# A state-space and expert layer on one Trainium2 core: five small moves in the order of a hand-scheduled loop

## The reference

```
h = layernorm(x) * (1 + ca) + sa
proj = h @ W_in.T;  x, gate = proj[:, :1024], proj[:, 1024:]
x = silu(conv_b + sum over 4 taps of conv_w * shifted x)
ssm = x @ W_x.T;  ts, B, C = rms(ssm[:, :32]), rms(ssm[:, 32:48]), rms(ssm[:, 48:])
dt = softplus(ts @ W_dt.T + b_dt)
state = state * exp(dt * A) + (dt * x) * B        # 1024 channels x 16 states, along the tokens
y = (sum over 16 states of state * C + x * D) * silu(gate);  out = y @ W_out.T
x = x + ga * out;  h = layernorm(x) * (1 + cb) + sb
x = x + gb * (h @ base_W.T + top-2 of 8 experts of rank 16)
```

## Time and profile before

| | |
|---|---|
| median of 3 runs | 1569.14 us (1564.22 to 1573.31) |
| the profiled execution's own time | 1564.21 us |
| its span | 1562.4 us |
| layer 1's recurrence, first to last scan | 536.4 to 1527.7 us of the span |
| granted PE clock, mean | 0.949 |
| busy share of the span, PE / DVE / ACT / POOL | 89% / 80% / 59% / 66% |

### The profile page before, as it was taken

The page is one execution under the profiler, slowest core; times in us unless marked ns, Lnnn a source line. Parts: engine busy times, 40 slices in busy tenths (PEclk is TensorE's granted clock), DMA queues, the critical chain, the costliest instruction groups (busy, mean ns, idle before and its releaser), DMA issues.

```text
span 1562.4 us, 25203 instructions
## 1 busy us (share of the span) xinstructions
PE 1384.7 (89%) x8789; PEld 995.4 (64%) x8789; DVE 1257.6 (80%) x1662; ACT 922.2 (59%) x2519; POOL 1038.6 (66%) x731
## 2 busy tenths in 40 slices
PE   6689999999999678699799899899899899988677
PEld 5467677767776467567567567567666666755543
DVE  4684674457344489999999999999999999999994
ACT  3332333223322677767877787787687777776651
POOL 0343242313223398888997997998898898899870
PEclk9699999999999889899999899999999999989589
DMA  9431222210001100200200110110020020020001
GB/s 326 163 109 55 88 83 74 66 38 20 29 28 33 68 14 1 82 1 15 68 28 15 55 42 1 56 54 1 24 86 1 14 96 1 1 68 28 1 0 41
DMA packets 32389, 77.17 MB, mean 49 GB/s; under 512 B 3667, under 2 KB 4723, under 8 KB 31750
## 3 DMA queue, kind: packets, MB, share of 16 engines
q1 hardware_dynamic: 32262, 75.55, 14.4%
HBM read 66.99 MB, written 8.55 MB: 48 GB/s over the span
## 4 chain that ended last, share of the span: by engine, by line
DVE 21%; PE 20%; POOL 10%; issue 9%; ACT 8%; DVEq 0%; ACTq 0%; POOLq 0%
DVE h L2212 12%; DVE acc L2228 6%; PE ps_h L1476 6%; POOL dbu L2024 5%; POOL h L2059 4%; ACT ps_a L1712 3%; PE ps_o L1500 2%; PE ps_m L1400 2%; ACT ab L1839 1%; PE ps_m L1440 1%; PE ps_h L1461 1%; PE ps_o L165 1%; PE ps_m L165 1%; DVE sg L2264 1%; PE ps_o L166 1%
## 5 line engine op out<-in xcount | busy, mean ns | idle before, releaser
L2212 DVE TENSOR_TENSOR_SCAN h<-ps_a,carry,dbu 128x512 f32<-128x512 f32 x512 | 626.3, 1266 | 14.5 <-ACT ps_a L1712 5.0
L2024 POOL TENSOR_TENSOR dbu<-dtu,b_all 128x1020 f32<-128x1020 f32 x256 | 598.6, 2358 | 27.1 <-DVE h L2212 27.1
L1712 ACT ACTIVATE ps_a<-dt,a_neg 128x256 f32<-128x256 f32 (+1 forms) x1024 | 443.2, 466 | 141.0 <-DVE h L2212 139.4
L1476 PE MATMUL ps_h<-ident,h 128*128 128x128 f32 x1536 | 228.3, 292 | 79.0 <-DVE acc L2228 66.9
L2228 DVE SCALAR_TENSOR_TENSOR acc<-ps_h,c_cur,acc 128x512 f32<-128x512 f32 x384 | 268.2, 738 | 9.9 <-PE ps_h L1476 9.4
L1476 PEld LDWEIGHTS ps_h<-ident,h 128*128 128x128 f32 x1536 | 183.8, 150 | 130.1 <-DVE h L2212 85.7
L714 POOL TENSOR_TENSOR hid_l<-hid,hid_h 128x256 f16<-128x256 f32 (+1 forms) x88 | 77.6, 885 | 156.2 <-ACT hid_h L605 156.1
L2059 POOL TENSOR_TENSOR h<-h,c_all 128x1024 f32<-128x1024 f32 x64 | 151.1, 2361 | 15.4 <-ACT carry L1732 15.4
L597 ACT ACTIVATE sil<-ps_gu 128x256 f32<-128x256 f32 (+1 forms) x88 | 34.0, 386 | 179.3 <-PE ps_gu L167 179.3
L165 PE MATMUL ps_m<-h_h,wi_h 128*128 128x256 f16 x432 | 119.1, 276 | 3.9 <-PEq L155 2.4
L166 PE MATMUL ps_m<-h_l,wi_h 128*128 128x256 f16 x432 | 118.6, 275 | 0.0
(11 more groups left out here) (392 smaller groups left out, 2864.0 us busy)
## 6 DMA issues: line engine op xcount, KB each, us to landing
b_all<-bt_scratch SPq DMA_DIRECT2D x32, 512.0 KB, 3.8
wm<-in_wmod SPq DMA_DIRECT2D x7, 1024.0 KB, 5.1
wo<-in_wmod SPq DMA_DIRECT2D x5, 1024.0 KB, 8.4
xa<-in_x SPq DMA_DIRECT2D x8, 512.0 KB, 4.5
stage<-in_W_in SPq DMA_DIRECT2D x4, 1024.0 KB
x_scratch<-x SPq DMA_DIRECT2D x8, 512.0 KB, 3.1
c_all<-bt_scratch SPq DMA_DIRECT2D x8, 512.0 KB, 6.1
x<-x_scratch SPq DMA_DIRECT2D x8, 512.0 KB, 3.6
```

The costliest lines, as they stand in the source:

```text
L1476: tr = pe.transpose(ps_h[:, t, j * P:(j + 1) * P], h[:, s % RING, j, t * P:(t + 1) * P], W["ident"][:])
L1712: ex = nc.scalar.activation(ps_a[:, j, j % 2:], dt[:, m, j % 2:], ACT.Exp, scale=a_neg[:, m, st:st + 1])
L2024: nc.gpsimd.tensor_tensor(dbu[:, s % AHEAD, :, 1:], dtu[:, :, 1:], b_all[:, st, 1:].unsqueeze(1).to_broadcast([P, DG, CH - 1]), ALU.mult). ...
L2212: nc.vector.tensor_tensor_scan(h[:, s % RING, two].rearrange("p j t -> p (j t)"), ps_a[:, two].rearrange("p j t -> p (j t)"), dbu[:, s % A ...
```

## The change

Nothing is added and nothing is removed; every instruction stays, in another place of its engine's program.

1. PE: `add_h` of the fourth weighed state moves in step 5 ahead of the output projection; `add_h` of the first weighed state of the second group moves in step 17 ahead of `turn_y` and W_x. (The fourth of the second group stays where it was.)
2. PE: gate tile 0 moves from step 17, ahead of W_x, to step 18, behind it and ahead of `turn_ss`.
3. PE: the first half of the base product of the experts (`experts(p, 0)`) moves from the middle of step 22 to the end of step 23, behind the turned states. In the last iteration it stays.
4. POOL: `rms_pow` moves ahead of the product of step 23.
5. ACT and DVE: `high` and `low` of `T3_AT` move one step earlier; in step 4 DVE's residual addition `add_out_projection(p, 0)` moves ahead of `make_sg(i, 6)` and of `low`.

```diff
-GA_AT = {17: (0,), 19: (1,), 28: (2, 3), 30: (4,), 31: (5,)}
+GA_AT = {18: (0,), 19: (1,), 28: (2, 3), 30: (4,), 31: (5,)}
-BASE_AT = {22: (0,), 24: (1,), 25: (2,), 26: (3,)}
+BASE_AT = {24: (1,), 25: (2,), 26: (3,)}
...
+                if s == JOIN_AT:
+                    add_h(i, KC - 1, first)
                 if p is not None and s:
                     for q in WO_AT.get(s, ()):
                         out_projection(p, q)
...
                 if n is not None:
                     for m in GA_AT.get(s, ()):
                         gate_tile(n, m)
+                if s == NS + 1:
+                    add_h(i, NS, first)
                 for m in YA_AT.get(s, ()):
                     turn_y(i, m)
...
-                if st in ADD_AT:
+                if st in ADD_AT and s not in (JOIN_AT, NS + 1):
                     add_h(i, s - st + ADD_AT[st], first)
...
                 if st == JOIN_AT + 2:
                     turn_h(i, s)
+                if p is not None and n is not None and s == NS + JOIN_AT + 2:
+                    experts(p, 0)
...
             if n is not None:
-                for t in at_slot(T3_AT, s):
+                for t in T3_AT.get(s, ()):
                     high(n - 1, t, S["t3_mm"], S["t3_hi"], h3_h, t3_bank(t))
...
                 db(i, s, first)
-                if n is not None and s == WX_AT + 6:
-                    rms_pow(n)
                 if s >= AHEAD - 1 and on_pool(s - (AHEAD - 1)):
                     weigh_h(i, s - (AHEAD - 1))
+                if n is not None and s == WX_AT + 5:
+                    rms_pow(n)
...
+                if p is not None and s == 4:
+                    add_out_projection(p, 0)
                 if s == 4:
                     make_sg(i, 6)
                 if n is not None:
-                    for t in at_slot(T3_AT, s, 2):
+                    for t in at_slot(T3_AT, s):
                         low(n - 1, t, S["t3_hi"], S["t3_lo"], h3_h, h3_l, t3_bank(t))
-                if p is not None and s == 4:
-                    add_out_projection(p, 0)
```

## The result

| | before | after |
|---|---|---|
| median of four runs each | 1570.34 us (1564.22 to 1573.31) | 1547.18 us (1545.25 to 1548.59) |
| ratio of the two, with its 95% interval | | 0.9865 [0.983, 0.99] |
| span of the profiled execution | 1562.4 us | 1544.7 us |
| granted PE clock, mean | 0.949 | 0.950 |

The kernel became faster by 1.35%. (The ratio is estimated from all runs; the quotient of the two medians is 0.9853.) Span against span it is 17.7 us, where the sum of the terms was 17.9.

The account below looks back on a forecast made before the run. DVE was taken as the bound, with only its idle time to win. The terms 10.5 + 4.2 + 1.4 + 1.8 = 17.9 us, taken off the median of 1569.1, gave 1551.2 us, range 1542 to 1567.

Parts of the forecast that it names:

- A: Steps 4 to 6, three moves: DVE's gaps of 1.44 us an iteration go, 10.5 us in all.
- B: POOL's power ahead of product 23: DVE no longer waits for the power, 4.2 us in all.
- C: Gate behind W_x, sum of state 16 ahead: W_x starts 0.2 us earlier an iteration, 1.4 us in all.
- D: Base product moved out of step 22: DVE's additions there wait less for PE, 1.8 us in all.
- All three moves are needed: Steps 4 to 6: moving `low` alone leaves most of its 1.27 us gap to the addition of step 4.
- A in iteration 0: Gap of 2.43 us before step 4's addition: 0.9 us won, since POOL's late weighed states hold the join.
- Both covers: Power ends about 872.2, before DVE arrives at 874.17; product 23 ends 1 us before scan 23 needs it.
- Covered, barely: PE's sum of state 17 would end at about 868.2, and the scan of step 21 needs it by 868.4.
- the 0.76 goes, and turning 22 at half clock gives some 0.25 back: Step 22: the addition's 0.76 us wait goes, and PE's half-clock turn of state 22 costs some 0.25 again.
- rivals 1 and 2: PE's clock stays low a little longer, 1557 us, chance 0.17; or PE bounds steps 23 and 24, 1581, 0.07.
- Rival 3: Gain taken back behind each gap, by POOL's weighing 19 or ACT in steps 4 to 6: 1564 us, chance 0.14.

Follow-up runs that it names:

- u_d: Changed kernel with the base product back in the middle of step 22; median 1545.82 us, ratio 0.9868 to the kernel before.
- u_a: Changed kernel with the fourth sum, residual addition, `high` and `low` of steps 4 to 6 put back; median 1560.11 us, ratio 0.9951 to the kernel before.
- u_b: Changed kernel with POOL's power behind the product of step 23 again; median 1553.70 us, ratio 0.9911 to the kernel before.
- u_c: Changed kernel with gate 0 and the sum of state 16 back in their old places; median 1548.98 us, ratio 0.9884 to the kernel before.
- a_sum: Kernel before with only the fourth sum moved ahead of the output projection in step 5; median 1559.59 us, ratio 0.9946 to the kernel before.
- u_lag: Changed kernel with only `high` and `low` one step later again; median 1551.08 us, ratio 0.9905 to the kernel before.
- a_lag: Kernel before with only `high` and `low` one step earlier; median 1572.22 us, ratio 1.0031 to the kernel before.
- d_22: Changed kernel with the base product one step earlier, at the end of step 22; median 1550.24 us, ratio 0.9894 to the kernel before.
- g_ud: Changed kernel with ACT's W_x copy between the decay halves of step 20 and the base product back in step 22; 1544.65 us, ratio 0.9866 to before.
- g_copy: Changed kernel with ACT's copy of W_x between the two halves of step 20's decays; median 1548.22 us, ratio 0.9874 to the kernel before.
- again: The changed kernel itself run once more, nothing changed; median 1550.22 us, ratio 0.9888 to the kernel before.

## Why the prediction was right, and where not

The forecast was 1551.2 us, in the range 1542 to 1567; 1547.18 was measured. The 4 us between come from the point it was counted from. The sum made 1546.3 for an execution like the one profiled, and 1546.5 is what the profiled one took. I then added the 4.9 us by which the median of before lay above its profiled execution; the median of after lies only 0.6 above its own.

Part by part, in us. The third column is read from the two traces: the waits of DVE at the places that a part is about, before less after. The last two are what undoing the part cost, in stretches of one profiled execution each:

| part | predicted | waits gone | undone: iteration 0 | undone: iterations 1 to 6 |
|---|---|---|---|---|
| A | 8.6 + 0.9 + 1.0 | 8.6 + 0.7 + 1.0 | 4.4 | 7.3 |
| B | 4.2 | 2.5 + 2.0 | 0.8 | 3.9 |
| C | 1.4 | 1.8 - 0.6 | -0.1 | 0.9 |
| D | 1.8 | -0.4 | (-0.4) | -1.1 |
| sum | 17.9 | 15.6 | 4.7 | 11.0 |
| before minus after | | 18.1 | 1.9 | 13.9 |

In "waits gone" the first number is iterations 1 to 6, the second iteration 0, the third iteration 7. D's -0.4 in iteration 0 is no cost of D, which has no instruction there; the changed kernel run again differs by as much.

The two ways of pricing do not agree, and the last two columns add up to 15.7 of 15.8 us by luck: 4.7 for 1.9 in one and 11.0 for 13.9 in the other. What undoing a part brings beside its own waits is, as far as the traces were followed, where the stretches at 1.2 GHz then fall, and POOL.

From iteration 7 to the end 1.0 was predicted and 2.3 came. A's 1.0 is there: the two waits of step 6 went from 0.75 and 1.07 us to 0.15 and 0.69. Undoing A, B or C costs 2.6 to 2.8 us there each time, and this is for the most part one place, the last output projection behind the last scan. In the changed kernel and in u_d no stretch at 1.2 GHz falls on it and it takes 7.03 us; in u_a, u_b and u_c one does, and it takes 8.25, 9.01 and 9.24. DVE waits 4.46 us for it in the changed kernel and 5.64, 6.39 and 6.63 in these. PE by time in the changed kernel:

```profile
1516.00 7.03 PE L1512 MATMUL ps_m<-wo,y 128*128 128x512 f32 x16
```

and in u_c:

```profile
1515.86 9.24 PE L1512 MATMUL ps_m<-wo,y 128*128 128x512 f32 x16
```

In the kernel before, DVE waited 5.61 us there, so part of the 2.3 us is where a stretch fell too.

- **A, 10.5: right in mechanism and size, 10.3.** Both gaps, 1.44 us, are gone from each of iterations 1 to 6. Undoing A costs less there (1.2 us each), since the additions of steps 21 and 22 wait 1.3 us less in u_a. Wrong was the sentence "All three moves are needed". The fourth sum alone takes away the whole 1.27 us (a_sum); the step I missed is that an earlier sum also frees `high`, which stands behind the join. I had read that in the earlier trace rows and still priced it only together with the others. Moving `high` and `low` is worth nothing in iterations 1 to 6 beside the other two (u_lag), and without the residual addition ahead it costs 7.3 us (a_lag).
- **A in iteration 0, 0.9: right.** The 2.43 us of before shrank to 1.71, as the late POOL had been allowed for. The 4.4 of u_a hold 2.4 of W_x at half clock, which the kernel before did not have.
- **B, 4.2: right, 4.5.** Both covers held, product 23 with 0.8 us in iteration 2 where 1 was named. That it would hold scan 23 by about 0.3 us in iteration 0 shows in u_c (0.37, for POOL's product); in the changed kernel the scan of step 21 waits ahead of it. The cost of undoing it in iterations 1 to 6, 3.9, is above the 2.5 of before, since DVE comes earlier now.
- **C, 1.4: right in size, 1.2.** W_x starts 0.3 us earlier and not 0.2, and the wait before scan 20 is 0.41 and not 0.5: 1.8 us in six iterations. "Covered, barely" for the scan of step 21 failed in iteration 0, where it waits 0.64 us and in u_c does not. The wait of 0.38 before the same scan in iteration 5 is not C's: u_c has it (0.36), and a_lag too (0.35), but no kernel with the late `high` has it. It is a small price of A's earlier `high`, and a wait of 0.29 us in step 20 went for it.
- **D, +1.8: it won nothing.** The step that failed is "the 0.76 goes, and turning 22 at half clock gives some 0.25 back". The 0.76 did go. But PE, without the base product, stood idle 2.44 us and turned step 22 in 1.94 us, and the addition of that step waited 0.61 us in iterations 1, 2, 3 and 6, of which 1 and 3 had only 0.15 before. In the earlier trace rows the clock had fallen ahead of the base product, and the 2.6 us saved rest on that; in u_d, with A, B and C in and the base product where it was, it ran at full clock (0.38 us a matmul instead of 0.59) and so did the turn behind it. D was priced against a state that the other parts do away with. It costs 1.1 us in iterations 1 to 6 (u_d, and d_22 the same; g_ud against g_copy 0.5) and not the 2.8 us of the additions, because POOL would take back most of that in the next iteration.

So the sum is right in part by luck. D's missing 2.2 us are made up by what was not forecast: DVE's own instructions took 1.7 us less in iterations 1 to 6 (720.96 us busy against 722.63), and the end 1.3 us less than A's part. On the rivals: the clock did not stay low longer (34.1 us at 1.2 GHz in iterations 1 to 6 against 44.4), so rivals 1 and 2 fell. Rival 3 fell for A and B. It was seen for C (iteration 0, and g_copy, where PE takes the gain back), and where more is won at steps 22 and 23 POOL takes it back before the addition of step 4, while rival 3 had named POOL's weighing for the second join.

The Trainium skill ("TensorE: Matmul & The Clock Gate", section "Why this matters for your kernels") asks to keep idle gaps out between bursts of matmuls. On the clock the runs side with it: with the base product in step 22, 13.7 us of six iterations are at 1.2 GHz (u_d) or 20.5 (d_22, in the very gap), and with it behind the turned states of step 23, 34.1. The gaps here are short, though: none of PE in iterations 1 to 6 of the changed kernel is over 2.45 us, and the clock falls all the same. On the time, by the same runs, it is worth 1.1 us there and at most 0.3 in all.

## What to carry to other kernels

In a loop bound by one in-order engine, list that engine's gaps and follow each to the instruction that is really late, past the one the profile names; here one sum moved ahead of a quarter of a projection was worth 7.8 of the 13.9 us won in iterations 1 to 6. Price each move of a set in the state that the others leave behind, not in the kernel before: that is where D went wrong, and where a_lag alone costs 0.3%. When more is won on that engine, look for the one that meets it next: POOL here, whose weighing shows only as a wait for "issue" on DVE and has to be followed back over PE. And compare from a fixed event ahead of the change to one behind it: two medians of the changed kernel differ by 3 us, the two stretches behind the first scan by 0.4.

## What the runs showed that I had not expected

- With a wait of PE longer by 0.6 us (1.89 against 1.29) its clock fell to 1.2 GHz in five of six iterations and not in the sixth (a_lag), for 3.4 us each time; with it scan 6 waits 1.4 to 1.7 us more (1.56 to 1.86 against 0.17). A clock that is a close thing makes a small wait dear.
- Where a stretch of 1.2 GHz falls decides what it costs: over W_x in iteration 0, 2.4 us (u_lag, u_a); over the last output projection, 1.2 to 2.2 us (u_a, u_b, u_c); over turned state 22, 0.5 us; 20 us of it in six iterations, 1.1 us (u_d).
- The start of layer 1's loop lies between 533.8 and 541.7 us in kernels whose layer 0 is the same program. The two latest (again, g_copy) had stretches at 1.2 GHz of 3.4 us near 500 and near 530, which the earliest ones had not; but u_b has both and starts at 537.6, and 5.1 of the 7.9 us between g_ud and g_copy are there before them (the same DVE instruction starts at 441.1 and 446.2 us). What makes the rest was not found.
